# Adaptive pooling, attention and a mixture of experts on one core: a score tile one unit earlier, a store on two queues, and three attention products out of rounded halves

## The chip, the core and the metric

The kernel runs on one core of a Trainium2 chip. The metric is the device time of one execution in microseconds (us), and the smaller the better. It has TensorE (PE in the profile), VectorE (DVE), ScalarE (ACT), GpSimd (POOL) and SyncE (SP, which here only starts transfers).

## The reference, cut to what matters

128 sequences of 32 tokens with 128 features go through a pooling, an attention and a mixture of experts, all in float32.

```
h  = pooled(x)                         # masked softmax pooling per sequence
q, k, v = h @ Wq, (h @ Wkv) @ Wk, (h @ Wkv) @ Wv          # 16 heads of 8
qr, kr  = rotary(h @ Wqr), rotary((h @ Wkv) @ Wkr)        # 32 wide, shared by all heads
w  = softmax(causal((q . k + qr . kr) / sqrt(40)))
x  = x + (w @ v) @ Wo
c2 = x @ W[category] + b[category]
tw = top 8 of 64 experts inside the top 4 of 8 groups of sigmoid(c2 @ gate), normalised, x 2.5
x  = x + sum over experts e of tw[e] * (silu(c2 @ Wg[e]) * (c2 @ Wu[e])) @ Wd[e] + shared expert
```

## The kernel before, in words

The 4096 tokens are worked in 8 blocks of 512 tokens (`NBLK`, `TOK`), tokens along the free side and features on the 128 partitions. A block of the expert part consists of 33 **units** (`UNITS`): 32 pairs of experts and, as unit 32, the shared expert. In unit p PE makes the gate product of pair p, the down product of pair p-4 and the up product of pair p. Each of these is `three(...)`: the float32 operand is held as two rounded halves (type float32r, names ending in `_hi` and `_lo`), and the product is hi·hi + lo·hi + hi·lo, three passes of 128x512.

For every unit the other engines do this: ACT takes the silu of the gate product in place (L552, `silu`). DVE multiplies it by the routing weights `cwb` (L1004) and by the up product (L1022), which gives `hid`. ACT rounds `hid` to `hid_hi` (L564, `rounded`), POOL subtracts to get `hid_lo` (L672), and four units later PE makes the down product. The gate product of unit p may start once DVE has done L1004 of unit p-2 (its bank is then free); unit 7 likewise waits for L1004 of unit 5.

The attention part of the next block is cut into 33 steps, and one of them is put behind each unit, on each engine, 5 steps ahead (`AHEAD`): behind unit p of expert block b stands step p+5 of attention block b+1, and behind units 28 to 32 stand steps 0 to 4 of attention block b+2. The places named further on:

- step 23 (unit 18): ACT copies the pooled tokens from PSUM to `h_feat` (L393, `pooled_out`);
- steps 22 to 29 (units 17 to 24): DVE's routing, a chain of small operations on `rt` and `biased` (`routing`, L814 to L857), of which L835, L838 and L847 are named in the rows;
- step 32 (unit 27): PE makes the rotary, query and key products of attention block b+2 out of `h_feat` (`first_products`), float32 operands, each one matmul of 128x512 that the profile shows as two records. This happens in expert blocks 0 to 5, for attention blocks 2 to 7. DVE turns the rotary product behind unit 28 (`rotate`) and spreads the keys behind units 29 to 32 (L725);
- steps 6 to 9 (units 1 to 4): DVE takes the four score tiles, adds the mask (L746) and takes the maximum (L748), and POOL subtracts it (L619). In expert block 0 this is moved by the table `TWO_TILES`, which DVE and POOL read, and by `SECOND_ROUND`, which PE reads: PE makes the scores of tiles 2 and 3 behind unit 4, DVE takes tile 0 ahead of unit 0, tile 1 behind unit 1, and tiles 2 and 3 behind unit 3. The up product of unit 6 waits until tile 2 has been read (`score_read`).

At the start, block 0 has its own order. The first routing weights are stored by ACT's queue to `cw_scratch` in two transfers (L465), one for each half of the rows. SP waits for both (`cw_stored`) and then loads the broadcast rows `cwb` one unit after the other (L362). In units 2 and 3 of block 0, L1022 multiplies `hid` by `cwb`, so both its inputs are in SBUF. ACT and POOL also split the expert weights into halves during block 0 (`split`, L480 and L631), one piece in each unit that the table `SPLITS` names: 6 to 16, and 18, 20, 22, 24, 26, 27.

```
TWO_TILES = {0: [], 1: [7], 2: [], 3: [8, 9], 4: []}
SECOND_ROUND = {1: [], 3: [], 4: [8]}
```

## Time and profile before

| | us |
|---|---|
| median of 3 runs | 715.75 |
| lowest and highest | 714.75, 717.88 |
| the profiled execution's own time | 716.17 |
| its span in the trace | 714.3 |
| PE busy in the span | 697.0 (98%) |
| DVE busy | 549.2 (77%) |
| ACT busy | 444.8 (62%) |
| POOL busy | 422.7 (59%) |

The profile shows one execution. The span is what the trace covers, from the first instruction to the last; the execution's own time has 1.9 us more around it. Busy time of an engine is the time in which it worked on an instruction, so what is missing is time in which it waited. Expert blocks 1 to 5 repeat with a period of 84.5 us; block 2 runs from about 224 to 308 us.

### The profile page before, as it was taken

The page shows a single profiled execution, that of the slowest core. Times are in us where ns is not written, and L with a number is a line of the kernel's source. Part 1 is how long each engine was busy: PE and PEld are TensorE (multiplying, and loading weights), DVE is VectorE, ACT ScalarE, POOL GpSimd, SP SyncE. Part 2 cuts the span into 40 slices and gives each one's busy share as a digit, 9 for nine tenths or more (in the row PEclk, how much of TensorE's full clock was granted, in tenths as well). Part 3 has the DMA queues.
Part 4 walks back from the last instruction along what each step waited for, and adds up shares of the span by engine and source line. Part 5 has one row for each costly group of instructions (what it writes and reads, how often), then busy time and mean ns, then how long its engine had stood idle before and what let it go on. Part 6 is the DMA issues. An engine that isn't in the chain of part 4 may idle for free.

```text
span 714.3 us, 15761 instructions
## 1 busy us (share of the span) xinstructions
PE 697.0 (98%) x5610; PEld 544.4 (76%) x5610; DVE 549.2 (77%) x1148; ACT 444.8 (62%) x858; POOL 422.7 (59%) x349
## 2 busy tenths in 40 slices
PE   9898998999999999999999999999999999999998
PEld 6665786777877778777787778777787777888886
DVE  5788669868788778887598866977878876887665
ACT  3878765686546855568455775558654685565554
POOL 3536887765555745566456654556555664666664
PEclk9998999999999999999999999999999999999999
DMA  8556334444453445436533463444564354346431
GB/s 280 166 199 151 120 114 110 114 148 105 128 140 99 147 116 116 130 99 172 119 103 120 136 147 106 131 111 138 112 129 138 97 153 119 108 124 153 128 131 51
DMA packets 65341, 92.96 MB, mean 130 GB/s; under 512 B 7728, under 2 KB 26928, under 8 KB 65264
## 3 DMA queue, kind: packets, MB, share of 16 engines
q1 hardware_dynamic: 61088, 86.96, 45.1%
q10 hardware_dynamic: 4176, 5.01, 2.0%
q8 instruction: 44, 0.72, 0.4%
q14 instruction: 33, 0.27, 0.1%
HBM read 88.40 MB, written 3.15 MB: 128 GB/s over the span
## 4 chain that ended last, share of the span: by engine, by line
PE 73%; DVE 12%; ACT 9%; issue 3%; POOL 1%; DMA 1%; DVEq 0%; ACTq 0%; SPq 0%; POOLq 0%
PE banks L1063 70%; DVE hid L1004 3%; DVE hid L1022 2%; ACT banks L552 2%; ACT s_t L432 2%; PE banks L1143 2%; DVE k_blk L725 1%; ACT L552 1%; ACT hid_hi L564 1%; ACT L432 1%; DVE pt_sb L700 1%; POOL hid_lo L672 1%; DMA cwb<-cw_scratch 1%; ACT pt_sb L377 1%; PE banks L1186 0%
## 5 line engine op out<-in xcount | busy, mean ns | idle before, releaser
L672 POOL TENSOR_TENSOR hid_lo<-hid,hid_hi 128x512 fp32r<-128x512 f32 x255 | 331.3, 1299 | 248.2 <-ACT hid_hi L564 246.4
L1004 DVE TENSOR_TENSOR hid<-banks,cwb 128x512 f32<-128x512 f32 x252 | 173.1, 687 | 111.0 <-ACT banks L552 109.8
L552 ACT ACTIVATE banks<-banks 128x512 f32<-128x512 f32 x252 | 146.2, 582 | 123.4 <-PE banks L1063 121.6
L564 ACT CAST hid_hi<-hid 128x512 fp32r<-128x512 f32 (+1 forms) x264 | 162.8, 616 | 79.9 <-DVE hid L1022 79.3
L1022 DVE TENSOR_TENSOR hid<-hid,banks 128x512 f32<-128x512 f32 (+1 forms) x262 | 179.8, 687 | 23.6 <-PE banks L1063 1.9
L1063 PE MATMUL banks<-c_hi,wg_hi 128*128 128x512 f32 x264 | 119.5, 453 | 5.9 <-DVE hid L1004 4.8
L1063 PE MATMUL banks<-hid_hi,wd_hi 128*128 128x512 f32 x264 | 104.1, 394 | 0.4 <-POOL hid_lo L672 0.2
L1063 PE MATMUL banks<-c_hi,wu_hi 128*128 128x512 f32 x256 | 102.3, 400 | 1.8 <-DVE hid L1022 1.6
L1063 PE MATMUL banks<-hid_hi,wd_lo 128*128 128x512 f32 (+1 forms) x264 | 104.0, 394 | 0.0
L1063 PE MATMUL banks<-c_hi,wg_lo 128*128 128x512 f32 x264 | 103.6, 392 | 0.0
L1063 PE MATMUL banks<-c_lo,wg_hi 128*128 128x512 f32 x264 | 103.5, 392 | 0.0
L1063 PE MATMUL banks<-c_lo,wu_hi 128*128 128x512 f32 x256 | 100.3, 392 | 0.0
L1063 PE MATMUL banks<-hid_lo,wd_hi 128*128 128x512 f32 x256 | 100.3, 392 | 0.0
L1063 PE MATMUL banks<-c_hi,wu_lo 128*128 128x512 f32 x256 | 99.9, 390 | 0.0
L1063 PEld LDWEIGHTS banks<-c_hi,wg_hi 128*128 128x128 f32 x264 | 49.8, 189 | 26.3 <-DVE hid L1004 8.6
L1063 PEld LDWEIGHTS banks<-c_hi,wu_hi 128*128 128x128 f32 x256 | 48.2, 188 | 17.3 <-DVE hid L1022 5.2
L1063 PEld LDWEIGHTS banks<-hid_hi,wd_lo 128*128 128x128 f32 (+1 forms) x264 | 49.7, 188 | 13.3 <-issue 2.7
L1063 PEld LDWEIGHTS banks<-hid_hi,wd_hi 128*128 128x128 f32 x264 | 49.7, 188 | 12.5 <-POOL hid_lo L672 0.9
L1063 PEld LDWEIGHTS banks<-c_lo,wg_hi 128*128 128x128 f32 x264 | 49.8, 189 | 10.9
L1063 PEld LDWEIGHTS banks<-c_hi,wg_lo 128*128 128x128 f32 x264 | 50.1, 190 | 8.7 <-issue 3.1
L1063 PEld LDWEIGHTS banks<-hid_lo,wd_hi 128*128 128x128 f32 x256 | 48.2, 188 | 10.8
L1063 PEld LDWEIGHTS banks<-c_lo,wu_hi 128*128 128x128 f32 x256 | 48.2, 188 | 10.6
(165 smaller groups left out, 814.8 us busy)
## 6 DMA issues: line engine op xcount, KB each, us to landing
cwb<-cw_scratch SPq DMA_DIRECT2D x254, 256.0 KB, 3.7
k_blk<-in_cond_w SPq DMA_DIRECT2D x112, 64.0 KB, 2.6
xf<-in_x_feat SPq DMA_DIRECT2D x7, 256.0 KB, 4.0
out_feat<-y ACTq DMA_DIRECT2D x7, 256.0 KB, 3.8
wg_raw<-in_we_gate SPq DMA_DIRECT2D x3, 512.0 KB, 8.3
wu_raw<-in_we_up SPq DMA_DIRECT2D x3, 512.0 KB, 9.0
wd_raw<-in_we_down SPq DMA_DIRECT2D x3, 512.0 KB, 8.8
xf<-in_x_tok SPq DMA_DIRECT2D x6, 256.0 KB, 2.7
```

The source lines that it names most:

```text
L377: nc.scalar.copy(pt_sb[:, t % 2, :], ((U[0], A1)[t % 2] if opening(blk) else A1)[:, :]).then_inc(S["probT_ready"], 1)
L432: nc.scalar.activation(s_t[:, t, :], s_t[:, t, :], ACT.Exp, scale=ATT_SCALE)\
L552: nc.scalar.activation(dst, gate_bank(p)[:, :], ACT.Silu).then_inc(S["silu_done"], 1)
L564: nc.scalar.copy(hid_hi[0:n, slot(b, p), :], hid[0:n, slot(b, p), :]).then_inc(S["hi_ready"], 1)
L672: nc.gpsimd.tensor_sub(rest, hid[0:n, slot(b, p), :], hid_hi[0:n, slot(b, p), :].bitcast(F32)).then_inc(S["lo_ready"], 1)
L700: last = nc.vector.tensor_mul(rot[:, i, :].rearrange("p (s t) -> p s t", t=SEQ), ps[rows, :].rearrange("p (s t) -> p s t", t=SEQ), C["rota ...
L725: nc.vector.tensor_scalar(k_blk[:, h, :], A1[:, :], C["head_of_group"][:, h:h + 1], None, ALU.mult)\
L1004: nc.vector.tensor_mul(hid[:, slot(b, p), :], gate_bank(p)[:, :], cwb[:, p % NCW, :])\
L1022: nc.vector.tensor_mul(hid[0:n, slot(b, p), :], hid[0:n, slot(b, p), :], up).then_inc(S["hid_ready"], 1)
L1063: return nc.tensor.matmul(dst, lhsT, rhs, **k)
L1143: last = nc.tensor.transpose(((U[0], A1)[t % 2] if opening(blk) else A1)[:, bass.ts(g, P)], probs, C["ident"])
```

## The change

There are three parts. The first moves attention step 8 (score tile 2) in expert block 0 from behind unit 3 to behind unit 2, on DVE and POOL. The second lets SP's queue store the second half of the rows of the first routing weights, while ACT's queue stores the first half; all later blocks are stored by ACT as before. The third makes the rotary, query and key products of attention blocks 2 to 7 with `three(...)`: behind unit 19 ACT rounds `h_feat` to `h_hi`, behind unit 20 POOL subtracts to get `h_lo`, and PE reads these two and the halves of the three weight matrices. Those are made once, in unit 19 of expert block 0, by three casts on ACT and three subtractions on POOL (128x128 each). The new tensors lie in memory that is free by then (`h_halves` over `s_t`, `w_halves` over `w`, and so on). The products of attention blocks 0 and 1 stay as they are.

```
--- before.py
+++ after.py
@@ -88,7 +88,9 @@
             return ctx.enter_context(nc.semaphore(name))
 
 
-        w = sb("w", [P, W_TOTAL])
+        with ExitStack() as first_form:
+            w = first_form.enter_context(nc.sbuf_tensor("w", [P, W_TOTAL], F32))
+        w_halves = sb("w_halves", [P, W_TOTAL], F32R)
         c = sb("c", [P, C_TOTAL])
         W = {n: w[:, a:a + k] for n, (a, k) in W_COLS.items()}
         C = {n: c[:, a:a + k] for n, (a, k) in C_COLS.items()}
@@ -110,8 +112,11 @@
         wg_hi, wu_hi = sb("wg_hi", [P, UNITS, P], F32R), sb("wu_hi", [P, NPAIR, P], F32R)
         wd_hi = sb("wd_hi", [P, UNITS, D], F32R)
         c_hi0, c_lo0 = sb("c_hi0", [P, TOK], F32R), sb("c_lo0", [P, TOK], F32R)
-        k_w, v_w = sb("k_w", [P, D]), sb("v_w", [P, D])
-        rope_w = sb("rope_w", [P, P])
+        with ExitStack() as first_form:
+            k_w = first_form.enter_context(nc.sbuf_tensor("k_w", [P, D], F32))
+            rope_w = first_form.enter_context(nc.sbuf_tensor("rope_w", [P, P], F32))
+        k_w_lo, rope_w_lo = sb("k_w_lo", [P, D], F32R), sb("rope_w_lo", [P, P], F32R)
+        v_w = sb("v_w", [P, D])
         vrep = sb("vrep", [P, TILES, SEQ])
         gbias = sb("gbias", [P, E])
         cat_row = sb("cat_row", [CATS, NSEQ], I32)
@@ -119,7 +124,14 @@
 
 
         xf = sb("xf", [P, TOK])
-        s_t = sb("s_t", [P, NG, TILES * HG * SEQ])
+        with ExitStack() as first_form:
+            s_t = first_form.enter_context(nc.sbuf_tensor("s_t", [P, NG, TILES * HG * SEQ], F32))
+        h_halves = sb("h_halves", [P, NG, TOK], F32R)
+        h_hi, h_lo = h_halves[:, 2, :], h_halves[:, 3, :]
+        FIRST = [rope_w[:, :], W["q"], k_w[:, :]]
+        halves_at = {n: w_halves[:, W_COLS[n][0]:W_COLS[n][0] + D] for n in ("kvT", "q", "k", "v")}
+        first_hi = [halves_at[n] for n in ("v", "kvT", "k")]
+        first_lo = [rope_w_lo[:, :], halves_at["q"], k_w_lo[:, :]]
         small = sb("small", [P, 16])
         h_feat = sb("h_feat", [P, TOK])
         q_sb = sb("q_sb", [P, TOK])
@@ -178,7 +190,7 @@
 
         S = {}
         for name in """cond_in consts_in proj_in prompt_in cats_in x_in0 x_in1 x_in2 xt_in0 xt_in1 xt_in blank pt_blank
-                vrep_ready row_in onehot_ready pool_chain pool_spread
+                h_hi_ready h_lo_ready first_split first_rest vrep_ready row_in onehot_ready pool_chain pool_spread
                 ws_in split_hi split_lo setup fold_ps folded cat_ps cat_read hidden_ps tanh_done score_ps pool_sub pool_exp
                 pool_prob pooled_ps pooled_ready
                 cwb_ps pick_ready res_in krope_in krope_ready wcat_in cw_stored y_free cwb_in0 cwb_in1 cwb_in2 cwb_in3
@@ -211,7 +223,7 @@
                 return [(step, 1) for step in moved[p]]
             return steps_in(p, b, last)
 
-        TWO_TILES = {0: [], 1: [7], 2: [], 3: [8, 9], 4: []}
+        TWO_TILES = {0: [], 1: [7], 2: [8], 3: [9], 4: []}
         SECOND_ROUND = {1: [], 3: [], 4: [8]}
 
         def pipeline(unit):
@@ -341,6 +353,9 @@
                 attention_loads(p, 1)
             for p in range(9, 13):
                 attention_loads(p, 1)
+            sp.wait_ge(S["cwT_ready"], 1)
+            sp.dma_start(cw_dram[:, 0:TOK].rearrange("e (u two n) -> e u two n", two=2, n=P)[:, :, 1, :],
+                         cw_feat[E:2 * E, :].rearrange("e (u n) -> e u n", n=P)).then_inc(S["cw_stored"], 16)
 
             def unit_loads(b, p, par, following, last, prev):
                 for step, blk in steps_in(p, following, last):
@@ -454,6 +469,9 @@
                                          scale=0.5).then_inc(S["score_ready"], 1)
                 elif p == 23 and 0 < blk < NBLK - 1:
                     pooled_out(blk + 1)
+                elif p == 24 and 0 < blk < NBLK - 1:
+                    act.wait_ge(S["pooled_ready"], blk + 2)
+                    nc.scalar.copy(h_hi, h_feat[:, :]).then_inc(S["h_hi_ready"], 1)
                 elif p == CWT:
                     act.wait_ge(S["cwT_ps"], blk + 1)
                     wait(act, "cw_stored", blk * 32)
@@ -461,7 +479,7 @@
                 elif p == CWT + 1:
                     dst = cw_dram[:, bass.ds(blk * TOK, TOK)].rearrange("e (u two n) -> e u two n", two=2, n=P)
                     act.wait_ge(S["cwT_ready"], blk + 1)
-                    for i in range(2):
+                    for i in range(1 if blk == 0 else 2):
                         act.dma_start(dst[:, :, i, :], cw_feat[E * i:E * i + E, :].rearrange("e (u n) -> e u n", n=P))\
                             .then_inc(S["cw_stored"], 16)
 
@@ -594,6 +612,10 @@
                     act.dma_start(out[:, bass.ds(b * TOK - TOK, TOK)], y[:, :]).then_inc(S["y_free"], 16)
                 if not prev and p in SPLITS:
                     split(SPLITS[p])
+                if not prev and p == 19:
+                    for dst, a in zip(first_hi, FIRST):
+                        last_split = nc.scalar.copy(dst, a)
+                    last_split.then_inc(S["first_split"], 1)
                 if p == X2_MOVED:
                     act.wait_ge(S["y_free"], b * 16 + 16)
                     nc.scalar.copy(y[:, :], x2_next[:, :]).then_inc(S["x2_moved"], 1)
@@ -618,6 +640,9 @@
                     s = s_t[:, t, :].rearrange("p (h k) -> p h k", k=SEQ)
                     nc.gpsimd.tensor_sub(s, s, head_max[:, t, :].unsqueeze(2).to_broadcast([P, TILES * HG, SEQ]))\
                         .then_inc(S["sub_tile"], 1)
+                elif p == 25 and 0 < blk < NBLK - 1:
+                    pool.wait_ge(S["h_hi_ready"], blk)
+                    nc.gpsimd.tensor_sub(h_lo, h_feat[:, :], h_hi.bitcast(F32)).then_inc(S["h_lo_ready"], 1)
                 elif p == 20:
                     pool.wait_ge(S["score_ready"], blk + 1)
                     nc.gpsimd.tensor_add(biased[:, :, :], score[:, :, :],
@@ -673,6 +698,11 @@
                                      hid_hi[0:n, slot(b, p), :].bitcast(F32)).then_inc(S["lo_ready"], 1)
                 if not prev and p in SPLITS:
                     split(SPLITS[p])
+                if not prev and p == 19:
+                    pool.wait_ge(S["first_split"], 1)
+                    for lo, hi, a in zip(first_lo, first_hi, FIRST):
+                        last_rest = nc.gpsimd.tensor_sub(lo, a, hi.bitcast(F32))
+                    last_rest.then_inc(S["first_rest"], 1)
                 for step, blk in steps_behind(p, following, prev, TWO_TILES, last):
                     if step == 1:
                         rope_add(blk)
@@ -1069,6 +1099,12 @@
                     pe.wait_ge(S["pool_sub"], 1)
                 pe.wait_ge(S["pooled_ready"], blk + 1)
                 wait(pe, "cwT_ready", blk)
+                if not isinstance(blk, int) or blk >= 2:
+                    pe.wait_ge(S["first_rest"], 1)
+                    pe.wait_ge(S["h_lo_ready"], blk - 1)
+                    for dst, hi, lo, name in zip((A0, A2, A1), first_hi, first_lo, ("rope_ps", "q_ps", "k_ps")):
+                        three(dst[:, :], hi, lo, h_hi, h_lo, True, True).then_inc(S[name], 1)
+                    return
                 mm(A0[:, :], rope_w[:, :], h_feat[:, :]).then_inc(S["rope_ps"], 1)
                 mm(A2[:, :], W["q"], h_feat[:, :]).then_inc(S["q_ps"], 1)
                 mm(A1[:, :], k_w[:, :], h_feat[:, :]).then_inc(S["k_ps"], 1)
```

How the order of instructions moves, at the places that matter. First POOL, from the last step of the gate scores (`biased`) to the addition of the rotary halves, in one of expert blocks 1 to 5. Before:

```order
L672 TENSOR_TENSOR hid_lo<-hid,hid_hi 128x512 x11
L623 TENSOR_TENSOR biased<-score,gbias 128x256
L672 TENSOR_TENSOR hid_lo<-hid,hid_hi 128x512 x14
L612 TENSOR_TENSOR rope_sum<-pt_sb 64x512
L672 TENSOR_TENSOR hid_lo<-hid,hid_hi 128x512 x2
```

And with the change:

```order
L697 TENSOR_TENSOR hid_lo<-hid,hid_hi 128x512 x11
L648 TENSOR_TENSOR biased<-score,gbias 128x256
L697 TENSOR_TENSOR hid_lo<-hid,hid_hi 128x512 x5
L645 TENSOR_TENSOR h_halves<-h_feat,h_halves 128x512
L697 TENSOR_TENSOR hid_lo<-hid,hid_hi 128x512 x9
L634 TENSOR_TENSOR rope_sum<-pt_sb 64x512
L697 TENSOR_TENSOR hid_lo<-hid,hid_hi 128x512 x2
```

The five `hid_lo` are those of units 16 to 20, and the new subtraction stands directly behind the one of unit 20.

Second PE, from the up product of unit 27 to the gate product of unit 28. Before:

```order
L1063 MATMUL banks<-c_lo,wu_hi 128x512
L1063 MATMUL banks<-h_feat,rope_w 128x512
L1063 MATMUL banks<-h_feat,w 128x512
L1063 MATMUL banks<-h_feat,k_w 128x512
L1063 MATMUL banks<-c_hi,wg_hi 128x512
```

And with the change:

```order
L1093 MATMUL banks<-c_lo,wu_hi 128x512
L1093 MATMUL banks<-h_halves,w_halves 128x512
L1093 MATMUL banks<-h_halves,rope_w_lo 128x512
L1093 MATMUL banks<-h_halves,w_halves 128x512 x5
L1093 MATMUL banks<-h_halves,k_w_lo 128x512
L1093 MATMUL banks<-h_halves,w_halves 128x512
L1093 MATMUL banks<-c_hi,wg_hi 128x512
```

Three float32 matmuls became nine of halves, in the same place.

Third DVE in units 2 to 4 of expert block 0. Before:

```order
L1022 TENSOR_TENSOR hid<-hid,cwb 128x512 x2
L746 TENSOR_TENSOR s_t<-banks,rope_mask 128x512
L748 TENSOR_REDUCE head_max<-s_t 128x16
L746 TENSOR_TENSOR s_t<-banks,rope_mask 128x512
L748 TENSOR_REDUCE head_max<-s_t 128x16
L1004 TENSOR_TENSOR hid<-banks,cwb 128x512
```

And with the change:

```order
L1052 TENSOR_TENSOR hid<-hid,cwb 128x512
L776 TENSOR_TENSOR s_t<-banks,rope_mask 128x512
L778 TENSOR_REDUCE head_max<-s_t 128x16
L1052 TENSOR_TENSOR hid<-hid,cwb 128x512
L776 TENSOR_TENSOR s_t<-banks,rope_mask 128x512
L778 TENSOR_REDUCE head_max<-s_t 128x16
L1034 TENSOR_TENSOR hid<-banks,cwb 128x512
```

Tile 2 now stands between the two multiplications of units 2 and 3.

## Rows read from the trace of the kernel before

**Rows 1.** the page of the kernel before, busy time of the engines

```profile
PE 697.0 (98%) x5610; PEld 544.4 (76%) x5610; DVE 549.2 (77%) x1148; ACT 444.8 (62%) x858; POOL 422.7 (59%) x349
```

**Rows 2.** the chain of waits, 262 to 310 us: start, us, what

```profile
267.77 24.53 PE banks L1063 x115
```

**Rows 3.** timeline of PE: start, us, what; idle time before it in brackets

```profile
285.13 0.39 PE L1063 MATMUL banks<-c_hi,wu_hi 128*128 128x512 f32 x1
...
289.70 0.39 PE L1063 MATMUL banks<-c_lo,wu_hi 128*128 128x512 f32 x1
...
294.30 0.40 PE L1063 MATMUL banks<-c_lo,wu_hi 128*128 128x512 f32 x1
...
297.34 0.39 PE L1063 MATMUL banks<-c_hi,wg_lo 128*128 128x512 f32 x1
```

**Rows 4.** timeline of ACT and DVE, 278 to 299 us

```profile
278.50 0.58 ACT L552 ACTIVATE banks<-banks 128x512 f32<-128x512 f32 x1
...
280.02 0.68 DVE L1004 TENSOR_TENSOR hid<-banks,cwb 128x512 f32<-128x512 f32 x1
...
298.61 0.69 DVE L1004 TENSOR_TENSOR hid<-banks,cwb 128x512 f32<-128x512 f32 x1 [2.15 <-ACT banks L552]
```

**Rows 5.** timeline of POOL and DVE where unit 20 of block 2 ends

```profile
283.01 1.29 POOL L672 TENSOR_TENSOR hid_lo<-hid,hid_hi 128x512 fp32r<-128x512 f32 x1 [1.50 <-ACT hid_hi L564]
284.53 0.18 DVE L835 TENSOR_SCALAR rt<-rt 128x32 f32<-128x32 f32 x1
285.21 0.42 DVE L838 TENSOR_TENSOR biased<-biased,rt 128x256 f32<-128x256 f32 x1
285.34 1.45 POOL L672 TENSOR_TENSOR hid_lo<-hid,hid_hi 128x512 fp32r<-128x512 f32 x1 [1.04 <-ACT hid_hi L564]
```

**Rows 6.** timeline of POOL and DVE at the same routing steps during block 0

```profile
113.42 1.29 POOL L631 TENSOR_TENSOR wd_lo<-wd_raw,wd_hi 128x512 fp32r<-128x512 f32 x1
113.69 1.06 DVE L835 TENSOR_SCALAR rt<-rt 128x32 f32<-128x32 f32 x1
114.67 1.27 POOL L672 TENSOR_TENSOR hid_lo<-hid,hid_hi 128x512 fp32r<-128x512 f32 x1
115.27 0.95 DVE L838 TENSOR_TENSOR biased<-biased,rt 128x256 f32<-128x256 f32 x1
```

**Rows 7.** timeline of DVE, PE's weight loads and POOL, 287 to 290 us

```profile
287.09 1.29 POOL L672 TENSOR_TENSOR hid_lo<-hid,hid_hi 128x512 fp32r<-128x512 f32 x1 [0.30 <-ACT hid_hi L564]
...
288.88 0.42 DVE L847 SCALAR_TENSOR_TENSOR rt<-rt,score 128x256 f32<-128x256 f32 x1
...
289.96 0.19 PEld L1063 LDWEIGHTS banks<-c_hi,wg_hi 128*128 128x128 f32 x1 [0.29 <-DVE hid L1004]
```

**Rows 8.** timeline of DVE, POOL and PE in the first units of block 0

```profile
58.74 0.69 DVE L1022 TENSOR_TENSOR hid<-hid,cwb 128x512 f32<-128x512 f32 x1 [1.50 <-DMA cwb<-cw_scratch]
60.30 1.71 DVE L1022 TENSOR_TENSOR hid<-hid,cwb 128x512 f32<-128x512 f32 x1 [0.86 <-DMA cwb<-cw_scratch]
61.93 0.68 DVE L746 TENSOR_TENSOR s_t<-banks,rope_mask 128x512 f32<-128x512 f32 x1
...
63.24 0.68 DVE L746 TENSOR_TENSOR s_t<-banks,rope_mask 128x512 f32<-128x512 f32 x1
...
65.95 0.69 DVE L1004 TENSOR_TENSOR hid<-banks,cwb 128x512 f32<-128x512 f32 x1
...
57.71 1.05 POOL L619 TENSOR_TENSOR s_t<-s_t,head_max 128x512 f32<-128x512 f32 x1
60.16 1.29 POOL L672 TENSOR_TENSOR hid_lo<-hid,hid_hi 128x512 fp32r<-128x512 f32 x1 [1.41 <-ACT hid_hi L564]
...
66.69 0.80 PE L1063 MATMUL banks<-c_hi,wg_hi 128*128 128x512 f32 x1 [3.07 <-DVE hid L1004]
```

**Rows 9.** timeline of ACT's DMA queue at the first store of routing weights

```profile
51.18 2.07 ACTq L465 DMA_DIRECT2D cw_scratch<-cw_feat  x2
```

**Rows 10.** windows: us, busy us of PE, PEld, DVE, ACT, POOL, granted clock, DMA, GB/s

```profile
64.00:74.00 10.00, 7.31 (x23) 5.83 (x24) 8.41 (x14) 8.91 (x16) 5.63 (x6) 0.66 0.67 177
```

More of the change, by code:

```diff
@@ L88, in sem @@
             return ctx.enter_context(nc.semaphore(name))
-        w = sb("w", [P, W_TOTAL])
+        with ExitStack() as first_form:
+            w = first_form.enter_context(nc.sbuf_tensor("w", [P, W_TOTAL], F32))
+        w_halves = sb("w_halves", [P, W_TOTAL], F32R)
         c = sb("c", [P, C_TOTAL])
@@ L121, in adaln_attention_moe @@
         xf = sb("xf", [P, TOK])
-        s_t = sb("s_t", [P, NG, TILES * HG * SEQ])
+        with ExitStack() as first_form:
+            s_t = first_form.enter_context(nc.sbuf_tensor("s_t", [P, NG, TILES * HG * SEQ], F32))
+        h_halves = sb("h_halves", [P, NG, TOK], F32R)
+        h_hi, h_lo = h_halves[:, 2, :], h_halves[:, 3, :]
+        FIRST = [rope_w[:, :], W["q"], k_w[:, :]]
+        halves_at = {n: w_halves[:, W_COLS[n][0]:W_COLS[n][0] + D] for n in ("kvT", "q", "k", "v")}
+        first_hi = [halves_at[n] for n in ("v", "kvT", "k")]
+        first_lo = [rope_w_lo[:, :], halves_at["q"], k_w_lo[:, :]]
         small = sb("small", [P, 16])
@@ L456, in attention_step @@
                     pooled_out(blk + 1)
+                elif p == 24 and 0 < blk < NBLK - 1:
+                    act.wait_ge(S["pooled_ready"], blk + 2)
+                    nc.scalar.copy(h_hi, h_feat[:, :]).then_inc(S["h_hi_ready"], 1)
                 elif p == CWT:
@@ L463, in attention_step @@
                     act.wait_ge(S["cwT_ready"], blk + 1)
-                    for i in range(2):
+                    for i in range(1 if blk == 0 else 2):
                         act.dma_start(dst[:, :, i, :], cw_feat[E * i:E * i + E, :].rearrange("e (u n) -> e u n", n=P))\
@@ L596, in unit @@
                     split(SPLITS[p])
+                if not prev and p == 19:
+                    for dst, a in zip(first_hi, FIRST):
+                        last_split = nc.scalar.copy(dst, a)
+                    last_split.then_inc(S["first_split"], 1)
                 if p == X2_MOVED:
@@ L620, in attention_step @@
                         .then_inc(S["sub_tile"], 1)
+                elif p == 25 and 0 < blk < NBLK - 1:
+                    pool.wait_ge(S["h_hi_ready"], blk)
+                    nc.gpsimd.tensor_sub(h_lo, h_feat[:, :], h_hi.bitcast(F32)).then_inc(S["h_lo_ready"], 1)
                 elif p == 20:
@@ L675, in unit @@
                     split(SPLITS[p])
+                if not prev and p == 19:
+                    pool.wait_ge(S["first_split"], 1)
+                    for lo, hi, a in zip(first_lo, first_hi, FIRST):
+                        last_rest = nc.gpsimd.tensor_sub(lo, a, hi.bitcast(F32))
+                    last_rest.then_inc(S["first_rest"], 1)
                 for step, blk in steps_behind(p, following, prev, TWO_TILES, last):
@@ L1071, in first_products @@
                 wait(pe, "cwT_ready", blk)
+                if not isinstance(blk, int) or blk >= 2:
+                    pe.wait_ge(S["first_rest"], 1)
+                    pe.wait_ge(S["h_lo_ready"], blk - 1)
+                    for dst, hi, lo, name in zip((A0, A2, A1), first_hi, first_lo, ("rope_ps", "q_ps", "k_ps")):
+                        three(dst[:, :], hi, lo, h_hi, h_lo, True, True).then_inc(S[name], 1)
+                    return
                 mm(A0[:, :], rope_w[:, :], h_feat[:, :]).then_inc(S["rope_ps"], 1)
```

14 lines of the change are left out of this document (10 added, 4 removed).

## The prediction

> **What bounds the kernel now.** The busy times come first: PE works 98% of the span and the next engine, DVE, 77% [rows 1]. So time is saved only where PE gets less work or waits less, and time is lost wherever PE is made to wait. The chain of waits of block 2 says where that is: from 267.8 to 292.3 us it stays on PE for 24.5 us [rows 2]. But PE is only just ahead there. In the timeline DVE's rows carry no idle time in front of them there [rows 5, 7], because the routing steps stand between its two multiplications of every unit, and at 289.96 PE's weight load for the next gate product has waited for DVE's L1004 [rows 7]. Up to there, what delays DVE hardly touches PE until its reserve is used up; from there on, DVE's delay is PE's delay, one for one. Behind the products of step 32 it is the other way round: DVE waits 2.15 us for ACT's silu, which waits for PE's gate product [rows 4]. So a shorter step 32 helps both engines. The third view is the opening of block 0, where PE stands idle for 3.07 us and is released by DVE's L1004 of unit 5 [rows 8].
>
> **Products out of halves, PE's side.** In a stream of passes of halves 20 steps take 289.70 - 285.13 = 4.57 us, so 0.228 us each [rows 3]. From the last pass ahead of the three float32 products to the second pass behind them are 297.34 - 294.30 = 3.04 us [rows 3]; less two passes that leaves 2.58 us for the three. Nine passes of halves take 9 x 0.228 = 2.06 us. The gain is 0.52 us, in each of expert blocks 0 to 5: **-3.1 us**, and it reaches the end since DVE too waits for PE there.
>
> **Products out of halves, ACT's side.** The new cast has the size of a silu (128x512), so I put it at the silu's 0.58 us. It stands ahead of the silu of unit 20, which starts at 278.50 and lasts 0.58; L1004 of unit 20 starts only at 280.02 [rows 4]. Even 0.58 us later the silu is done at 279.7. That costs nothing; without that cover it would be up to 0.6 us a block. In block 0 three casts of 128x128 come on top, with the same cover.
>
> **Products out of halves, POOL's side.** This is the term that decides. The new subtraction follows `hid_lo` of unit 20 on POOL, which ends at 283.01 + 1.29 = 284.30, and its input is long there; it is of the same shape as that one, so it runs from 284.3 to 285.6. `hid_lo` of unit 21 would start at 285.6 instead of 285.34, which matters to nobody (four units of reserve). But DVE has L835 at 284.53 and L838 at 285.21 in that stretch, 0.18 and 0.42 us long [rows 5], all operands in SBUF. Block 0 shows the same steps with POOL busy without a break, for there a piece of weight splitting stands behind `hid_lo`: POOL works from 113.42 to 114.71 and from 114.67 to 115.94, and L835 takes 1.06 and L838 0.95 us; both end right after POOL's instruction [rows 6]. That is 0.88 + 0.53 = 1.41 us more for DVE, in the same geometry: a subtraction that begins 0.25 us ahead of L835, and another behind it. The bounds: 0 if the two don't collide in blocks 1 to 5; 0.88 if only L835 is caught; 1.41 if both are. I take 1.41, since L838, once shifted to 286.1, falls into `hid_lo` of unit 21 (285.6 to 286.9). The Trainium skill ("SBUF — State Buffer", section "Who interferes with whom") says that DVE and GpSimd share a pair of ports under an exclusive lock, and that a DVE instruction with two SBUF inputs, or one in a 2-port mode, waits for a GpSimd instruction that reads SBUF to end. By that rule too both would be held, and without it, if they only shared bandwidth, the sum would fall to that of the first rival below.
>
> PE's reserve is then used up: at 289.96 it is zero [rows 7], so PE loses 1.41 us in each of blocks 1 to 5, and nothing after that gives it back: **+7.0 us**. In block 0, L838 is held by `hid_lo` of unit 21 already; now the new subtraction holds it instead, over the same time (114.7 to 116.0). The three small subtractions fall into 110.7 to 112.0, where POOL stood idle. Block 0 costs about 0.
>
> **Third tile one unit earlier.** DVE waits for `cwb` ahead of both multiplications, 1.50 and 0.86 us; then come two tiles, 63.24 - 61.93 = 1.31 us apart, and L1004 of unit 5 ends at 66.64, with PE behind it at 66.69 [rows 8]. With tile 2 ahead of the multiplication of unit 3 it lies in the wait, partly. The multiplication takes 1.71 us instead of 0.69 because POOL's `hid_lo` runs until 61.45 [rows 8]; a start at 60.7 instead of 60.3 changes nothing in its end at 62.0. So the tile's 1.31 us leave the path: **-1.3 us**. What is late next is again L1004 of unit 5. At worst the multiplication ends 0.4 later and 0.9 is left.
>
> **Store on two queues.** ACT's queue issues the two transfers one behind the other, in 2.07 us [rows 9]; side by side the last starts at most half of that, 1.0 us, earlier, and `cwb` lands as much earlier. But the multiplication of unit 2 at 58.74 starts when POOL's L619 ends, 57.71 + 1.05 = 58.76 [rows 8], and that one stays. Bounds 0 and 1.0; I take **-0.1**. SP's wait costs nothing, its queue has nothing else to start before the store.
>
> **TensorE's clock in the opening.** From 64 to 74 us the granted clock is 0.66 on average [rows 10], which is 6.8 us at 1.2 GHz instead of 2.4, after the idle time of 3.07 us. PE worked 7.31 of these ten us, so it worked at least 4.1 of the 6.8, and half of what it worked is lost: 2.0 to 3.4 us. The idle time shrinks to some 2.3 us (the up product of unit 6 no longer waits for tile 2, so it begins earlier too). Whether the clock still falls, and for how long, no row tells: 0 to 3.4 us come back. I take **-1.0**, nearer to the case in which it falls, as 2.3 is near 3.07.
>
> **Sum.** 716.2 (the profiled execution's own time, 0.4 over the median of 715.75) - 3.1 + 7.0 - 1.3 - 0.1 - 1.0 = 717.7. Against the median of the runs that is **717.3**. With the clock term at its ends, 714.9 to 718.3. All changes under 0.5% (3.6 us, about what a measurement of this kernel can tell from no change) count as the same.
>
> **Rivals.**
> - *No collision (22%).* POOL's new subtraction finds DVE elsewhere, or DVE's delay is absorbed: 715.75 - 3.1 - 1.3 - 0.1 - 1.0 = 710.2, faster by 0.8%. For it: POOL is idle for 1 us or more ahead of most `hid_lo` [rows 5]. Against it: these gaps are where DVE now runs its SBUF steps, and block 0 has paid.
> - *Half a collision (13%).* Only L835 is held: 0.88 x 5 = 4.4 instead of 7.0, so 714.7. The same.
> - *A third step is caught (11%), slower.* L847 starts at 288.88, 0.51 us after POOL's `hid_lo` that began at 287.09 has ended [rows 7]. If DVE's delay makes that `hid_lo` late by 0.5 us more than L847, L847 waits too, and L835's row shows that such a wait costs up to 0.88: 1.41 + 0.88 = 2.3 us in each of five blocks, 11.4 in all, so 715.75 - 5.5 + 11.4 = 721.7, +0.8%. From a total delay of 1.8 us a block on, the result is slower by over 0.5%. Against it: both follow from the same L1022, so they shift together.
> - *The opening gives nothing back (within the first case).* Where the clock falls as before and the tile saves 0.9 us, 718.7.
>
> **Chances.** The forecast has 54%, and nearly all of it lies within 0.5%; the half collision adds 13% there. The first rival gives 22% of faster, the third 11% of slower; a clock that stays up with a cheaper collision adds a little to faster, one that stays low with a dearer one to slower. So faster 0.25, same 0.60, slower 0.15. The range must take in the first rival to hold 8 in 10: 709.8 to 719.6; the forecast's own is 714.9 to 718.7.
>
> **What would show it.** In block 2 after: `h_halves` on POOL begins within 0.1 us of the end of `hid_lo` of unit 20; L835 lasts about 1.0 and L838 about 0.9 us in all of blocks 1 to 5, not only in block 0; PE shows idle time of over 1 us in units 24 to 26, released by L1004; the period of 84.5 us becomes 85.4. The nine passes lie 0.23 us apart, and DVE's wait behind them is 1.6. In the opening PE's idle time is about 2.3 us and gate 7 starts near 65.3. The forecast is wrong if L835 and L838 keep 0.18 and 0.42 us, or if they grow and the period does not.

## The result, and the profile after

| | before | with the change |
|---|---|---|
| median, us | 714.50 (20 runs) | 717.36 (20 runs) |
| lowest and highest | 710.64, 717.88 | 716.45, 718.71 |
| the profiled execution's own time | 716.17 | 717.06 |
| its span | 714.3 | 715.1 |

The ratio of the times is 1.0045, with a 95% interval of 1.0034 to 1.0057: 0.45% slower, so "within 0.5%", and 0.06 us from the forecast of 717.3. The median of before that the forecast stood on, 715.75 from three runs, has become 714.50 over 20. So the change was forecast to cost 1.6 us and costs 2.9 between medians, and that the time itself was met so closely is in part luck (below). Between the two profiled executions it is 0.9 us, 0.8 by their spans, since before's (716.17) was 1.7 us above its median. That is a matter of the opening, and has experiments below.

The page, where it answers to [rows 1], and the windows view that answers to [rows 10] (the same columns):

```profile
PE 695.0 (97%) x5628; PEld 544.2 (76%) x5628; DVE 556.3 (78%) x1148; ACT 447.6 (63%) x867; POOL 430.9 (60%) x358
```

```profile
64.00:74.00 10.00, 8.18 (x69) 6.39 (x70) 9.15 (x14) 9.71 (x18) 5.64 (x6) 1.00 0.63 176
```

PE has 2.0 us less work and DVE is busy 7.1 us longer with as many instructions as before. Longer instructions, not more of them: that is the trace of a collision. The granted clock is 1.00 where it was 0.66.

**Where the time went.** DVE's `c_lo` (L957 before, L987 after) comes once a block and divides the trace into periods:

| from one `c_lo` to the next | before | after | difference |
|---|---|---|---|
| first copy to `h_feat`, from the start | 12.66 | 12.28 | -0.4 |
| first period (the opening and block 0 up to unit 26) | 83.46 | 80.33 | -3.1 |
| five periods, each with the steps of units 20 and 21 of one of blocks 1 to 5, and the products of the block before it | 84.42 to 84.50 | 85.35 to 85.47 | +4.7 in all |
| seventh period (the products of block 5, no new subtraction) | 83.55 | 83.12 | -0.4 |

Together +0.8 us, the difference of the spans; the two stretches left out, up to the first `c_lo` and behind the last, differ by less than 0.1 us each. A steady block has become 0.95 us longer. Two of the rows behind the table, from DVE's timeline after, are 85.38 us apart:

```profile
205.98 0.68 DVE L987 TENSOR_TENSOR c_lo<-c,c_hi 128x512 fp32r<-128x512 f32 x1
...
291.36 0.68 DVE L987 TENSOR_TENSOR c_lo<-c,c_hi 128x512 fp32r<-128x512 f32 x1
```

**The collision**, block 2 after, timeline of POOL and of DVE, to be held against [rows 5]:

```profile
279.90 1.29 POOL L697 TENSOR_TENSOR hid_lo<-hid,hid_hi 128x512 fp32r<-128x512 f32 x1 [1.50 <-ACT hid_hi L582]
281.15 1.31 POOL L645 TENSOR_TENSOR h_halves<-h_feat,h_halves 128x512 fp32r<-128x512 f32 x1
282.42 1.29 POOL L697 TENSOR_TENSOR hid_lo<-hid,hid_hi 128x512 fp32r<-128x512 f32 x1
```

```profile
281.42 1.08 DVE L865 TENSOR_SCALAR rt<-rt 128x32 f32<-128x32 f32 x1
282.41 0.68 DVE L1034 TENSOR_TENSOR hid<-banks,cwb 128x512 f32<-128x512 f32 x1
283.01 0.97 DVE L868 TENSOR_TENSOR biased<-biased,rt 128x256 f32<-128x256 f32 x1
```

L865 (L835 before) begins 0.27 us into the new subtraction and ends 0.04 us behind it (282.50 against 282.46). L868 (L838 before) then falls into the next `hid_lo`, and ends 0.27 us behind that. L1034 between them, which reads a PSUM bank, lasts 0.68 us as ever, with POOL busy beside it. The view of one line's instructions (least, median and most ns) says that it is so in all blocks and no accident of this one:

```profile
L865 DVE TENSOR_SCALAR rt<-rt x8: 174/1079/1090, 45.3 to 622.2; 128x32 f32<-128x32 f32 x8
```

```profile
L868 DVE TENSOR_TENSOR biased<-biased,rt x8: 418/966/980, 45.6 to 622.9; 128x256 f32<-128x256 f32 x8
```

**PE behind it**, timeline of PE after, idle time in brackets:

```profile
282.45 0.39 PE L1093 MATMUL banks<-c_lo,wu_hi 128*128 128x512 f32 x1
283.15 0.50 PE L1093 MATMUL banks<-c_hi,wg_hi 128*128 128x512 f32 x1 [0.31 <-DVE hid L1034]
...
286.01 0.50 PE L1093 MATMUL banks<-c_hi,wg_hi 128*128 128x512 f32 x1 [0.28 <-DVE hid L1034]
...
288.31 0.50 PE L1093 MATMUL banks<-c_hi,wg_hi 128*128 128x512 f32 x1
288.65 0.40 PE L1093 MATMUL banks<-c_hi,wg_lo 128*128 128x512 f32 x1
...
292.87 0.39 PE L1093 MATMUL banks<-h_halves,w_halves 128*128 128x512 f32 x1
...
294.91 0.39 PE L1093 MATMUL banks<-c_hi,wg_hi 128*128 128x512 f32 x1
```

A pass of halves normally starts 0.23 us after the one before it; the gate product at 283.15 starts 0.70 after it, released by L1034. A second gate product waits at 286.01, 0.68 after the pass ahead of it, and a third, at 288.31, starts 0.34 after. These are units 24 to 26. From 282.45 to 288.65 twenty steps take 6.20 us, where twenty of before took 4.57 [rows 3]. So PE pays for DVE's delay here, 0.45 us at each of two gate products and the rest in steps of about 0.1, and the row's idle time in brackets shows less than what is lost. The nine passes of halves take 294.91 - 292.87 = 2.04 us where the three float32 products took 2.58 [rows 3]. Behind them DVE waits less than in [rows 4]:

```profile
296.41 0.69 DVE L1034 TENSOR_TENSOR hid<-banks,cwb 128x512 f32<-128x512 f32 x1 [1.58 <-ACT banks L570]
```

**The opening**, timelines of DVE, POOL and PE after, against [rows 8]:

```profile
57.70 1.17 DVE L1052 TENSOR_TENSOR hid<-hid,cwb 128x512 f32<-128x512 f32 x1 [0.89 <-DMA cwb<-cw_scratch]
...
60.11 1.34 DVE L1052 TENSOR_TENSOR hid<-hid,cwb 128x512 f32<-128x512 f32 x1
```

```profile
59.61 1.29 POOL L697 TENSOR_TENSOR hid_lo<-hid,hid_hi 128x512 fp32r<-128x512 f32 x1 [1.28 <-ACT hid_hi L582]
```

```profile
64.81 0.50 PE L1093 MATMUL banks<-c_hi,wg_hi 128*128 128x512 f32 x1 [2.11 <-DVE hid L1034]
...
70.69 0.52 PE L1179 MATMUL banks<-c,s_t 128*128 128x128 f32 x3 [1.01 <-ACT pt_sb L392]
```

Gate 7 starts at 64.81 instead of 66.69; counted from the first copy to `h_feat`, since the starts of the two executions differ, 52.5 instead of 54.0, 1.5 us earlier. PE's idle time ahead of it is 2.1 instead of 3.1 us. But there is a new idle time of 1.0 us at 70.69, which before did not have. The chain of waits of the changed kernel shows what leads there:

```profile
60.11 1.35 DVE hid L1052
61.46 0.02 issue
61.48 0.62 ACT hid_hi L582
62.10 0.49 ACT banks L570
62.59 0.02 issue
62.61 1.28 ACT L447
63.89 0.01 issue
63.90 1.67 ACT s_t L447 x3
...
67.14 1.28 ACT L570
...
70.03 0.52 ACT pt_sb L392
70.55 0.14 issue
70.69 0.63 PE banks L1179 x4
```

From the end of unit 3's multiplication to the transposes of PE the path runs through ACT alone, with two pieces of 1.28 us that name no tensor, ahead of the first exponential (L447) and again ahead of the next silu (L570). The third tile does not lie on this path.

### The profile page after: what moved, and what is told of

Its sections match the earlier page's. It is cut to its first block, busy times and chain, and to the rows that moved or that the text cites. A ratio compares the mean times of both kernels' runs of the same rounds, so it can differ in the third digit from the quotient of the medians.

```text
span 715.1 us, 15821 instructions
## 1 busy us (share of the span) xinstructions
PE 695.0 (97%) x5628; PEld 544.2 (76%) x5628; DVE 556.3 (78%) x1148; ACT 447.6 (63%) x867; POOL 430.9 (60%) x358
## 4 chain that ended last, share of the span: by engine, by line
PE 62%; DVE 19%; ACT 11%; issue 6%; DMA 1%; POOL 1%; DVEq 0%; SPq 0%; POOLq 0%
PE banks L1093 59%; DVE hid L1034 6%; DVE hid L1052 3%; ACT banks L570 3%; ACT s_t L447 2%; PE banks L1179 2%; ACT L570 1%; DVE k_blk L755 1%; ACT L447 1%; DVE pt_sb L730 1%; ACT hid_hi L582 1%; DVE rt L865 1%; DVE biased L868 1%; DVE rt L850 1%; DVE rt L853 1%
## 5 line engine op out<-in xcount | busy, mean ns | idle before, releaser
L1034 DVE TENSOR_TENSOR hid<-banks,cwb 128x512 f32<-128x512 f32 x252 | 172.9, 686 | 106.9 <-ACT banks L570 105.7
L570 ACT ACTIVATE banks<-banks 128x512 f32<-128x512 f32 x252 | 146.1, 582 | 121.3 <-PE banks L1093 119.6
L1093 PE MATMUL banks<-c_hi,wg_hi 128*128 128x512 f32 x264 | 117.6, 445 | 6.8 <-DVE hid L1034 5.7
L1093 PEld LDWEIGHTS banks<-c_lo,wu_hi 128*128 128x128 f32 x256 | 48.1, 188 | 10.6
```

The source lines that it names most:

```text
L570: nc.scalar.activation(dst, gate_bank(p)[:, :], ACT.Silu).then_inc(S["silu_done"], 1)
L1034: nc.vector.tensor_mul(hid[:, slot(b, p), :], gate_bank(p)[:, :], cwb[:, p % NCW, :])\
L1093: return nc.tensor.matmul(dst, lhsT, rhs, **k)
```

## The experiments

Each was timed beside the kernel before, in three sessions in which that had a median of 713.70 to 713.72 (21 to 29 runs). The ratios are against those runs, and can differ by 0.001 from the quotient of the two medians. "Period" is the median of the five steady ones, from `c_lo` to `c_lo`. In before, e1 and e8, which leave the steady blocks alone, it is 84.43 to 84.48, and 84.45 stands for it below.

| run | median | ratio, 95% interval | period |
|---|---|---|---|
| e1, tile alone | 712.24 | 0.9987 (0.9962 to 1.0012) | 84.45 |
| e2, store alone | 711.93 | 0.9978 (0.9964 to 0.9992) | 84.5 |
| e3, halves alone | 718.39 | 1.0070 (1.0045 to 1.0094) | 85.4 |
| e5, halves made, not used | 721.29 | 1.0120 (1.0084 to 1.0155) | 85.9 |
| e6, halves without POOL's part | 710.12 | 0.9952 (0.9933 to 0.9971) | 83.9 |
| e4, subtraction at unit 18 | 708.58 | 0.9937 (0.9916 to 0.9957) | 83.7 |
| e7, subtraction at unit 21 | 711.13 | 0.9965 (0.9952 to 0.9978) | 84.1 |
| e10, e4 without the tile | 708.61 | 0.9937 (0.9917 to 0.9958) | 83.8 |
| e8, before, PE kept busy | 712.93 | 0.9996 (0.9983 to 1.0010) | 84.4 |
| e9, e4 and e8 together | 708.36 | 0.9939 (0.9919 to 0.9959) | 83.7 |
| e11, e10 and e8 together | 708.43 | 0.9929 (0.9902 to 0.9956) | 83.7 |

### The three parts, each alone

e1 is the kernel before with one line changed, e2 with the store by SP and ACT, e3 the change without these two.

```
-        TWO_TILES = {0: [], 1: [7], 2: [], 3: [8, 9], 4: []}
+        TWO_TILES = {0: [], 1: [7], 2: [8], 3: [9], 4: []}
```

> The kernel before with score tile 2 of block 0 behind unit 2, nothing else. Theory (the tile leaves the path of L1004 of unit 5, and the shorter idle time keeps TensorE's clock up more often): gate product 7 starts 1.3 us earlier against the start of the block, at about 65.3, PE's idle time ahead of it is 2.1 to 2.3 us instead of 3.07; the time is 1.3 us less where the clock does as in the kernel before, and up to 4 less where it stays up: median 711.5 to 713.5. Rival (the tile was hidden anyway, all of the gain ahead of block 1 is the clock's): gate product 7 starts within 0.3 us of where it was.

> The kernel before with the second half of the first routing weights stored by SP's queue, nothing else. Forecast theory (the multiplication of unit 2 is held by POOL's subtraction anyway): 0.1 us off the path, time within 0.3 of before. Rival, from the trace of the change against that of the tile alone (the rows cwb land about 0.8 us earlier, and both multiplications follow): gate product 7 starts 0.5 to 0.8 us earlier against the copy of h_feat than in a kernel without it, and the time is 0.5 to 0.8 us less where the clock does the same.

> The change's third part alone on the kernel before: products out of halves, no tile moved, store on one queue. Theory (POOL's subtraction holds L835 and L838 in blocks 1 to 5): -0.52 x 6 + 1.41 x 5 = +3.9 us over the kernel before, period of blocks 1 to 5 about 85.4 us. Rival (the products out of halves are no cheaper on PE, and POOL costs nothing): period 84.5 to 84.7, time within 1 us of before.

e1: gate 7 begins 53.1 us after the copy to `h_feat`, 0.9 us earlier than before, but the time can't be told from no change. Nor is it the tile's alone (see e10). e2 gives 1.6 us by its ratio (0.6 to 2.6 by the interval), more than the 0.1 of the forecast. e3 carries the whole loss: +0.70%, a period of 85.4 as in the full change. The product of the three ratios is 1.0035, and the whole change measured 1.0045 (1.0034 to 1.0057), so the parts account for it within the noise.

A likely reason for the store's gain shows beside e3. Timelines of DVE and POOL at the multiplication of unit 3, first of e2:

```profile
59.44 0.69 DVE L1025 TENSOR_TENSOR hid<-hid,cwb 128x512 f32<-128x512 f32 x1 [0.39 <-DMA cwb<-cw_scratch]
```

```profile
59.78 2.75 POOL L675 TENSOR_TENSOR hid_lo<-hid,hid_hi 128x512 fp32r<-128x512 f32 x2 [1.28 <-ACT hid_hi L567]
```

and of e3:

```profile
59.77 0.69 DVE L1049 TENSOR_TENSOR hid<-hid,cwb 128x512 f32<-128x512 f32 x1 [0.71 <-DMA cwb<-cw_scratch]
```

```profile
59.78 3.07 POOL L694 TENSOR_TENSOR hid_lo<-hid,hid_hi 128x512 fp32r<-128x512 f32 x2 [1.41 <-ACT hid_hi L579]
```

In before that multiplication began 0.14 us after POOL's `hid_lo` and took 1.71 us [rows 8]. In e2 the rows of `cwb` land earlier, it begins 0.34 us ahead of POOL, and takes 0.69. In e3, whose store is the old one, it begins 0.01 us ahead, and takes 0.69 as well: there it is POOL that is held, two `hid_lo` taking 3.07 us instead of 2.6. One microsecond of one engine or the other hangs on which of the two comes first. Both orders occur with the old store, and with the new one as well: in e11, which has the new store and the tile behind unit 3, the multiplication begins 0.02 us behind. So that the store settles the order more often is likely, and not shown.

### Cost and gain of the halves, apart

Both of these have the tile and the store of before; the edits are against the change. e5 makes the halves of `h_feat`, waits for them, and still multiplies in float32; so it has the cost without the gain. e6 leaves POOL's subtraction out, and its third pass takes `h_hi` again, so the low half of h is missing from three products: the gain without the cost.

```
 e5
                 pe.wait_ge(S["h_lo_ready"], blk - 1)
-                for dst, hi, lo, name in zip((A0, A2, A1), first_hi, first_lo, ("rope_ps", "q_ps", "k_ps")):
-                    three(dst[:, :], hi, lo, h_hi, h_lo, True, True).then_inc(S[name], 1)
-                return
 e6
-                    nc.gpsimd.tensor_sub(h_lo, h_feat[:, :], h_hi.bitcast(F32)).then_inc(S["h_lo_ready"], 1)
...
-                        three(dst[:, :], hi, lo, h_hi, h_lo, True, True).then_inc(S[name], 1)
+                        three(dst[:, :], hi, lo, h_hi, h_hi, True, True).then_inc(S[name], 1)
```

> The kernel before with the cast to h_hi on ACT (unit 19) and the subtraction to h_lo on POOL (unit 20) in blocks 0 to 5, but float32 products as before, which wait for the subtraction; the halves are not read by anyone and the weights are not split. Theory: only the cost is left, 1.41 x 5 = +7.0 us over the kernel before (6.0 to 8.0), period 85.9 us. Rival (PE's nine passes are what costs): 0 to +0.5 us, period 84.5.

> The kernel before with the products of blocks 2 to 7 out of halves, but without POOL's subtraction of h: the third pass takes h_hi again instead of h_lo, so the low half of h is left out of the rotary, query and key products and the result differs. All nine passes, the cast and the split of the weights remain. Theory: only PE's gain is left, -0.54 us a block, so 3.2 us less than the kernel before, period of blocks 1 to 5 about 83.9 us. Rival (the products out of halves are what costs): period 84.5 or more.

e5's period is 1.49 us longer than 84.45, e6's 0.53 shorter (83.92 on the mean of the last four; its first, right behind the opening, is 84.34). Together +0.96, and the change has +0.95: cost and gain are separate and add up. Times six and five, 713.7 + 5 x 1.49 = 721.2 (measured 721.29) and 713.7 - 6 x 0.53 = 710.5 (measured 710.12). ACT's cast is in both, and e6's gain is the full 0.53, so the cast costs nothing. In e5 the lines of L835 and L838 stand under other numbers, with the same durations as in the change:

```profile
L853 DVE TENSOR_SCALAR rt<-rt x8: 173/1082/1092, 45.2 to 626.2; 128x32 f32<-128x32 f32 x8
```

```profile
L856 DVE TENSOR_TENSOR biased<-biased,rt x8: 416/962/975, 45.4 to 626.8; 128x256 f32<-128x256 f32 x8
```

### Is it the work or its place?

A rival says that POOL simply has 1.3 us more to do in each block. Then it wouldn't matter where the subtraction stands. e4 casts and subtracts right behind the copy to `h_feat`, at unit 18; e7 moves the subtraction alone, one unit later. Both are edits of the change.

```
 e4
                 elif p == 23 and 0 < blk < NBLK - 1:
                     pooled_out(blk + 1)
-                elif p == 24 and 0 < blk < NBLK - 1:
                     act.wait_ge(S["pooled_ready"], blk + 2)
                     nc.scalar.copy(h_hi, h_feat[:, :]).then_inc(S["h_hi_ready"], 1)
...
-                elif p == 25 and 0 < blk < NBLK - 1:
+                elif p == 23 and 0 < blk < NBLK - 1:
                     pool.wait_ge(S["h_hi_ready"], blk)
 e7
-                elif p == 25 and 0 < blk < NBLK - 1:
+                elif p == 26 and 0 < blk < NBLK - 1:
```

> The changed kernel with the rounding of h_feat directly behind its copy (unit 18 instead of 19) and POOL's subtraction behind hid_lo of unit 18 instead of 20. There it begins at about 280.0 of the kernel before's time, where DVE's L823 is held by POOL already, and POOL is idle again when L835 comes. Theory (the place collides, not the work): L835 and L838 back to 0.18 and 0.42 us in blocks 1 to 5, period 83.9 to 84.1 us, time 717.4 - 7 = 710.4, from 709.5 to 711.5. Rival (POOL's 1.3 us cost DVE wherever they stand, or PE waits for something else): period 85.0 or more, 716 to 718.

> The changed kernel with POOL's subtraction for h_lo one unit later, behind hid_lo of unit 21 instead of 20; the cast stays. By the rule that a held operation ends right after POOL's, read off the trace of the changed kernel: L835 and L838 (their counterparts) back to 0.18 and 0.42 us, hid_lo of unit 22 late by 1.0 us and the score multiplication behind it (L847 before) held in its place, 0.8 to 1.0 us instead of 0.42. Period 84.1 to 84.5 us, so 711.5 to 713 us. Rival (every place costs 1.4): period 85.4, 717.

The same work at unit 18 turns +0.45% into -0.63%. Line view, timelines of POOL and DVE in block 2 of e4:

```profile
L864 DVE TENSOR_SCALAR rt<-rt x8: 172/178/319, 44.7 to 613.0; 128x32 f32<-128x32 f32 x8
```

```profile
274.54 1.30 POOL L644 TENSOR_TENSOR h_halves<-h_feat,h_halves 128x512 fp32r<-128x512 f32 x1
275.81 1.30 POOL L696 TENSOR_TENSOR hid_lo<-hid,hid_hi 128x512 fp32r<-128x512 f32 x1
```

```profile
274.55 0.68 DVE L1033 TENSOR_TENSOR hid<-banks,cwb 128x512 f32<-128x512 f32 x1
275.15 0.74 DVE L852 TENSOR_TENSOR rt<-rt 128x32 f32<-128x32 f32 x1
275.93 0.69 DVE L1051 TENSOR_TENSOR hid<-hid,banks 128x512 f32<-128x512 f32 x1
```

L864 is back at 0.18 us. During the first half of the new subtraction DVE is on L1033, which is not held. L852 is held until the subtraction ends, but it was held by a `hid_lo` in the kernel before already (L823 there, median 940 ns), and now for 0.2 us less. So the period is 84.45 - 0.53 - 0.2 = 83.7. I had expected 83.9 to 84.1, without these 0.2, and 709.5 to 711.5 us, where 708.58 came. In e7 another step is caught, the one that was L847 before:

```profile
L877 DVE SCALAR_TENSOR_TENSOR rt<-rt,score x8: 419/702/1020, 48.4 to 621.7; 128x256 f32<-128x256 f32 x8
```

It takes 0.70 instead of 0.42, and the period follows: 84.45 - 0.53 + 0.28 = 84.2, measured 84.1. I had expected 0.8 to 1.0 for it, and 711.5 to 713 us, where 711.13 came. Three places of one instruction give three prices: 1.49, 0.2 and -0.2 us a block.

### What the tile is worth

e10 is e4 with tile 2 put back behind unit 3.

> The changed kernel with the halves of h at unit 18 on both engines, and score tile 2 back behind unit 3. Compared with the same kernel with the tile behind unit 2 (708.6). Theory from the traces (the tile's gain ahead of gate product 7 is given back in units 7 and 8, where PE then stands 1.0 us): within 0.8 us of 708.6 either way. Rival (the tile is worth its 1.3 us): 709.7 to 710.5.

708.61 against e4's 708.58: between medians the tile is worth nothing. But it settles the order of unit 3's multiplication and POOL's `hid_lo`. In the profiles of the change, e1, e4, e7 and e9, all with the tile ahead of it, the multiplication begins 0.5 us behind POOL's and takes 1.3 us, never 0.7. In e10's, timelines of DVE and POOL, it begins 0.36 us ahead:

```profile
59.09 0.69 DVE L1051 TENSOR_TENSOR hid<-hid,cwb 128x512 f32<-128x512 f32 x1 [0.37 <-DMA cwb<-cw_scratch]
```

```profile
59.45 2.74 POOL L696 TENSOR_TENSOR hid_lo<-hid,hid_hi 128x512 fp32r<-128x512 f32 x2 [1.28 <-ACT hid_hi L581]
```

From the profiles, in us, the third and fourth column counted from the first copy to `h_feat`; "low clock" is the time at 1.2 GHz in the opening, and the last column goes from the first `c_lo` to the second:

| profile: tile, store | multiplication against POOL's | its end | gate 7 | low clock | first period |
|---|---|---|---|---|---|
| before: old, old | 0.14 behind | 49.4 | 54.0 | 6.8 | 83.5 |
| e1: new, old | 0.51 behind | 49.7 | 53.1 | 3.4 | 81.6 |
| e3: old, old | 0.01 ahead | 48.1 | 52.8 | none | 79.6 |
| e2: old, new | 0.34 ahead | 47.7 | 52.3 | none | 79.5 |
| e10: old, new | 0.36 ahead | 47.7 | 52.3 | none | 79.0 |
| e4: new, new | 0.51 behind | 49.2 | 52.5 | none | 80.3 |
| change: new, new | 0.50 behind | 49.2 | 52.5 | none | 80.3 |

e3 has the opening of before, and its gate 7 comes 1.2 us earlier by the order alone. e10 and e4 differ in the tile alone: gate 7 starts at the same time within 0.2 us, but e10's multiplication ends 1.5 us earlier, PE doesn't wait for `pt_sb` (in e4 it is idle for 0.98 us at 70.05), and the first period is 1.3 us shorter. The times of all executions fit, sorted afterwards by their mean granted clock: six of e10's ten have 0.999 or 1.000 and take 707.9 us on the mean, the other four 710.2; of e4's twelve ten have it, and take 708.7. So the tile seems to make the kernel steadier and its best executions slower, by some 0.9 us, and in the median the two cancel. These are few executions, and the sorting was not planned.

### What the clock is worth, and why before scatters

Ahead of gate 7 of block 0 PE multiplies into a free bank once tile 3 is read; nothing uses the products.

```
                ahead = not prev and p in (2, 3)
+                if not prev and p == 7:
+                    pe.wait_ge(S["score_read"], 2 * TILES)
+                    warm(10, A1)
```

> The kernel before with ten 128x128 products of the identity into a free bank while PE waits for gate product 7 of block 0 (behind the reading of tile 3); they end ahead of the gate product. Theory (the idle time there lowers TensorE's clock in some runs, which costs them 1.5 to 3 us): no stretch at 1.2 GHz inside the block, median 711 to 712.5, and no run over 714.5. Rival (the spread of the kernel before comes from the transfers at the start): median within 0.5 of before, spread unchanged.

> The changed kernel with the halves of h at unit 18 on both engines, and the ten products while PE waits for gate product 7. Theory: the moved halves give 708.6 and the clock was up there in the trace already, so 707.5 to 708.6, with no run over 709.5. Rival: the added products delay gate product 7 or the transposes, 709 or more.

> The kernel of the run before this one, with the ten products while PE waits for gate product 7. If the clock is what makes the no-tile kernel slower in some runs, the spread shrinks and the median is at or under that of the run without them, 707.5 to 708.6; if the warming products stand in the way in the runs in which the wait is short, it is up to 1 us above.

Windows of e8 and of e5, which has no such products and a clock low for part of that stretch:

```profile
64.00:74.00 10.00, 9.71 (x85) 7.89 (x85) 9.00 (x15) 9.64 (x18) 6.36 (x6) 1.00 0.59 163
```

```profile
64.00:74.00 10.00, 7.72 (x60) 6.21 (x61) 9.00 (x15) 9.64 (x18) 6.34 (x6) 0.83 0.60 175
```

A clock of 0.66 over these ten us is 6.8 us at 1.2 instead of 2.4 GHz [rows 10], one of 0.83 is 3.4 us. From the copy to `h_feat` to the second `c_lo` the kernel before took 111.4 us, e5 109.3, e6 108.6 (with 3.4 us at the low clock like e5) and e8 108.0; in all four unit 3's multiplication is held. So by these single executions, which differ in a little more than the clock, 6.8 us at the low clock cost 3.4 us, and 3.4 us cost 0.6 to 1.2.

But e8's median is 712.93 against 713.72, and by the ratio no difference can be told; I had expected 711 to 712.5. Each execution's mean granted clock is on record and shows more. It is 0.999 or 1.000 in the profiles without a low stretch in the opening, 0.998 in those with 3.4 us and 0.995 in before's with 6.8. Of the 76 executions of before in the three sessions, 18 have 0.999 or 1.000 and take 711.7 us on the mean, 30 have 0.998 and take 713.7, and 28 have less and take 714.8. All eleven of e8 have 0.999 or 1.000. So the clock does fall in some executions of before and not in others, and the extra products keep it up. Yet e8's mean is 712.9, and not 711.7. The order of unit 3's multiplication can be the rest: in e8's profile it is held, and in the profiles in which it comes first PE's idle time ahead of gate 7 is 1.8 us and the clock stays up, so that the fast executions of before may be those. That is not shown, as only profiles show the order. The 29 runs of before in e8's session spread from 710.4 to 715.2 us, e8's eleven from 712.0 to 713.9. Thirteen of the 29 lie above e8's longest, so its long times are gone; only three lie below 712, too few to say that the short ones are gone too. In e9 and e11 the extra products bring nothing that can be measured over e4 and e10.

## Why the prediction was right, point by point

- *Products out of halves, PE's side*, -0.52 us a block: -0.53 in e6's periods and -0.54 in the change's row. Right.
- *ACT's side*, 0: right (e6).
- *POOL's side*, +1.41 a block from block 0's rows [rows 6]: L865 +0.90 and L868 +0.55, 1.45 in DVE's rows and 1.49 in e5's periods. Right in mechanism and size. All of DVE's delay reaches PE, as PE's reserve of zero [rows 7] said. That neither step ends before POOL's instruction does, and that L1034 with its PSUM input between them isn't held, agrees with the exclusive lock of "SBUF — State Buffer", section "Who interferes with whom", in the Trainium skill. It speaks against shared bandwidth, which would have slowed L1034 or left L865 shorter. Whether L865, which has one input tile, was held because of a 2-port mode, no run shows. The rival *no collision* and *half a collision* fall by L865's and L868's rows. *A third step is caught* falls too: L877's median after is 417 ns. e7 shows that the rival's step was the right one to fear, at 0.28 us for it rather than 0.88.
- *PE's idle time*: expected over 1 us, in units 24 to 26, released by L1034. Units and releaser are right, the form only partly: the brackets show 0.31 and 0.28 us, and the rest of the 1.6 us lies in passes that start late (above).
- *Third tile*, -1.3: **this term failed**. The rows named for it came out: gate 7 came 1.5 us earlier and PE's wait fell from 3.1 to 2.1 us (I had said 65.3 and 2.3). But e10 against e4 measures 0.0 us between medians. The step that failed is "what is late next is again L1004 of unit 5". Late next was ACT's chain to `pt_sb`, which starts at the end of unit 3's multiplication. The tile, put ahead of that multiplication, could not make its end earlier, and where `cwb` came in time to be ahead of POOL it made it later, by 1.5 us in the profiles of e4 and e10. The prediction took the 1.71 us of the multiplication as given; it was 0.69 in e2, e3 and e10.
- *Store*, -0.1: too small. e2 measures -0.22% (0.08 to 0.36), 1.6 us. I had bound the gain of an earlier `cwb` at unit 2's multiplication, where POOL stood in the way, and not asked the same at unit 3's, where coming earlier than POOL is worth a whole microsecond. Part of the 1.6 us is the clock's: ten of e2's twelve executions have a mean granted clock of 0.999 or 1.000, against six of before's 29 beside it.
- *Clock*, -1.0 out of 0 to -3.4: between the two profiled executions it was the far end, -3.4, since before's was one with 6.8 us at the low clock and after's had none. Between medians it must be less, as many runs of before have no low stretch or a short one. The nearest to a measurement is e8, which keeps the clock up in every execution: 0.3 us by the ratio (-0.7 to 1.2), 0.8 by the medians. So the -1.0 is neither confirmed nor excluded. In the change's twenty executions the clock hardly matters: fourteen have 0.999 or 1.000 and take 717.4 us on the mean, the other six 717.6.
- *Sum*: the steady part was forecast at 7.0 - 3.1 = +3.9 and is 5 x 1.49 - 3.1 = +4.3. The opening was forecast at -2.4, and the medians leave 2.9 - 4.3 = -1.4 for it. So the opening was taken 1.0 us too well and the steady part 0.4. That the sum still met the time within 0.1 is luck: its base, the median of three runs of before, was 1.25 us above that of 20, and the errors cancel. What was right is the sign, the mechanism and the size of the steady part; the whole change was forecast at +1.6 us and is +2.9.

The better kernel follows from the mechanism. With the subtraction at unit 18 (e4) the time is 708.6 us, 0.6% below before (0.4 to 0.8), and by the two ratios (1.0045 / 0.9937) the change is 1.1% slower than it.

## What to carry to other kernels

Before giving GpSimd an instruction that reads SBUF, look at what VectorE does in exactly that stretch of the timeline: beside a product with a PSUM input it was free, and beside a 0.18 us step on a 128x32 tile it cost 0.9 us. Where VectorE is within a microsecond of the bound, the place of such an instruction is a parameter to try, and was worth some 8 us here (1.1%), more than the 3.2 us of the products it served. And when work is moved off the path in front of one wait, follow the other paths that start at the same event: here the one through ScalarE to `pt_sb` took back what the tile gave in front of gate 7.
